# Tower of 16 pairs written out, with keys in SBUF, router results in the projections' bank, one numbered order of PSUM uses and a new order on four engines

## The reference, cut to what matters

```
x = emb[tokens] * sqrt(128) + positions                       # layer 1: additive attention
q, k, v = x @ Wq + bq, x @ Wk + bk, x @ Wv + bv
scores = einsum('d,bijd->bij', attn_scale, tanh(q[:, :, None, :] + k[:, None, :, :]))
x = layer_norm(x + softmax(scores) @ v @ Wo + bo)
x = layer_norm(x + relu(x @ W1 + bf1) @ W2 + bf2)
h = layer 2: causal attention of 8 heads, added to x
h = _ln(x); logits = (h @ Wr) @ codebook.T / 0.7              # layer 3: 64 experts, 2 of them for each token
out = residual + ffn(ln(mixture of 2 experts + shared expert))
```

## Time and profile before

| what | value |
|---|---|
| median of 3 runs | 871.07 us (868.9 to 873.77) |
| span of the profiled execution | 867.1 us |
| its own time | not listed apart from these runs |
| first add of the tower to last add | 12.6 to 544.9 us |
| tower without adds, up to the counts | 544.9 to 626 us |
| experts and last layer | 626 to 867.1 us |
| DVE, ACT, PE busy | 75%, 75%, 89% of the span |

### The profile page before, as it was taken

The page is one execution under the profiler, slowest core; times in us unless marked ns, Lnnn a source line. Parts: engine busy times, 40 slices in busy tenths (PEclk is TensorE's granted clock), DMA queues, the critical chain, the costliest instruction groups (busy, mean ns, idle before and its releaser), DMA issues. The chain is left out here.

```text
span 867.1 us, 22473 instructions
## 1 busy us (share of the span) xinstructions
PE 774.3 (89%) x7235; PEld 593.5 (68%) x7235; DVE 653.6 (75%) x2152; ACT 651.1 (75%) x1487; POOL 324.3 (37%) x396
## 2 busy tenths in 40 slices
PE   2777998888989999999899998988889999999898
PEld 1454676565756766667666675665679999999787
DVE  5999989979999999999999999654533334443685
ACT  3787999979898988998988989766335555565354
POOL 3110322425333353343433533444424645554211
PEclk9999999999999999999999999998899999999999
DMA  3459999999999989898898898997079999996411
GB/s 96 121 110 193 205 188 206 197 189 211 190 197 210 192 195 206 175 211 180 181 208 179 188 197 180 210 185 166 26 228 378 377 395 402 338 363 216 153 30 37
DMA packets 81344, 175.77 MB, mean 203 GB/s; under 512 B 8053, under 2 KB 34764, under 8 KB 81281
## 3 DMA queue, kind: packets, MB, share of 16 engines
q1 hardware_dynamic: 65104, 162.23, 76.1%
q0 software_dynamic: 5664, 7.92, 2.8%
q10 hardware_dynamic: 10512, 4.83, 2.0%
HBM read 63.95 MB, written 113.14 MB: 204 GB/s over the span
## 5 line engine op out<-in xcount | busy, mean ns | idle before, releaser
L893 DVE TENSOR_TENSOR arena<-qT,b_qk 128x2304 f32<-128x2304 f32 x128 | 323.7, 2543 | 1.6 <-DVE v_bias L918 0.3
L624 ACT ACTIVATE arena<-arena 128x2304 f32<-128x2304 f32 x128 | 271.6, 2123 | 35.0 <-DVE arena L893 34.0
L1334 PE MATMUL b_s<-arena,apad 128*32 128x192 f32 x3072 | 159.4, 343 | 27.0 <-ACT p L633 18.5
L1334 PEld LDWEIGHTS b_s<-arena,apad 128*32 128x32 f32 x3072 | 89.8, 113 | 83.9 <-issue 42.0
L779 ACT ACTIVATE act_h<-big,arena 128x128 f32<-128x128 f32 x324 | 92.4, 368 | 72.2 <-PE big L1654 65.6
L544 POOL TENSOR_TENSOR kept<-kept,rs 96x384 f32<-96x384 f32 x64 | 52.6, 823 | 212.6 <-DVE rs L1028 212.4
L592 POOL DMA_INDIRECT eo_dram<-gT,toff x81 | 79.0, 976 | 89.9 <-issue 56.0
L676 ACT ACTIVATE kept<-kept,mx 96x96 f32<-96x96 f32 x256 | 92.3, 365 | 14.5 <-DVE mx L1021 14.5
L1654 PE MATMUL big<-hbT,arena 128*128 128x128 f32 x648 | 86.7, 277 | 6.4 <-DMA arena<-in_wpack 2.4
L1654 PEld LDWEIGHTS big<-hbT,arena 128*128 128x128 f32 x648 | 78.8, 192 | 8.1 <-issue 6.3
L1208 DVE TENSOR_SCALAR hbT<-b_t,cols 128x128 f32<-128x128 f32 x81 | 33.2, 410 | 62.1 <-PE b_t L1647 58.3
(11 more groups left out here) (207 smaller groups left out, 1422.4 us busy)
## 6 DMA issues: line engine op xcount, KB each, us to landing
rows_dram<-act_h SPq DMA_DIRECT2D x32, 3096.0 KB
arena<-in_wpack SPq DMA_DIRECT2D x81, 578.0 KB
prT<-rows_dram ACTq DMA_DIRECT2D x73, 64.5 KB
arena<-eo_dram SPq DMA_DIRECT2D x4, 512.0 KB, 8.1
x_dram<-res SPq DMA_DIRECT2D x16, 96.0 KB
out<-of SPq DMA_DIRECT2D x12, 128.0 KB, 1.8
eo_dram<-gT,toff POOLq DMA_INDIRECT x81
rows_dram<-rows_now,slot_now POOLq DMA_INDIRECT x64
```

The source lines that it names most:

```text
L624: act.activation(v, v, ACT.Tanh).then_inc(s["tanh"], 1)
L893: dve.tensor_tensor(ring[c % TRING].rearrange("p (x m n) -> p x m n", m=CQ, n=N), qv.unsqueeze(3).to_broadcast([D, SPLIT * QG, CQ, N]), kv ...
L1334: last = pe.matmul(b_s[32 * a:32 * a + 32, 0:SPLIT * N], apad[:, 31 - line:63 - line], t[:, :, a, m, :], start=(line == 0), stop=(line == ...
```

## The change

1. **Written out.** `in_turns` calls `body(n)` for all n from -4 to 20; the `Fori` over pairs is gone on PE, ACT, DVE and POOL, and with it register-valued waits and most of the `gate`s (a wait with a semaphore increment of its own behind it). SP keeps its loops. The scatter's slots of all pairs have a column each (`slots`), and the gathers read their index straight from `eidx`, without the copy into `eidx_now`.
2. **Keys in SBUF.** A new ACT stage `keys` copies the 128x192 keys to `kT` with their bias; `queries` on DVE copies the queries behind it. Both tensors have two buffers. `add` reads two SBUF operands. `qk` of the next pair waits for `queries` and no longer for the adds.
3. **Router results in `b_qk`.** Logits and ranks move from `b_y` to `b_qk`.
4. **Banks in a round.** The uses of the three large banks are numbered in PE's order, use i takes bank i mod 3 and waits until use i - 3 has been read. The uses of `b_t` and of `b_y` wait in the same way, each for the use before it.
5. **New orders** on PE, ACT, DVE and POOL, below. The shared expert's first tiles also move.

```diff
-            def qk_evac(p):
-                dve.wait_ge(s["qk"], p + 1)
-                wait(dve, s["add"], p * CH)
-                dve.tensor_scalar(qT[:, :], b_qk[:, 0:TN], bqk[:, :], None, ALU.add).then_inc(s["qk_ev"], 1)
-                dve.wait_ge(s["qk_ev"], p + 1)
+            def queries(p):
+                dve.wait_ge(s["keys"], p + 1)
+                dve.tensor_scalar(qT[:, p % 2, :], p_q, bq, None, ALU.add).then_inc(s["queries"], 1)
 
             def add(p, c):
+                if c == 0:
+                    dve.wait_ge(s["queries"], p + 1)
                 wait(dve, s["score"], p * CH + c - TRING + 1)
                 g, cc = c // CPB, c % CPB
-                kv = p_k[:, g * N:(g + 1) * N]
+                kv = kT[:, p % 2, g * N:(g + 1) * N]
...
+            def keys(p):
+                wait(act, s["add"], (p - 1) * CH)
+                act.wait_ge(s["qk"], p + 1)
+                act.activation(kT[:, p % 2, :], p_k, ACT.Identity, bias=bk).then_inc(s["keys"], 1)
...
-        p_lg = b_y[0:N, 288:288 + G * E].rearrange("p (g e) -> p g e", g=G)
+        p_lg = b_qk[0:N, 0:G * E].rearrange("p (g e) -> p g e", g=G)
...
             def keep_rows(p):
-                if not (known(p) and p == 0):
-                    gate(pool, s["scat"], p * 16 * G * TOPK)
-                gate(pool, s["tn"], p + 1)
+                wait(pool, s["scat"], p * 16 * G * TOPK)
+                pool.wait_ge(s["tn"], p + 1)
...
+            def big_bank(p, what):
+                sem, uses = bank_free(p, what)
+                if uses:
+                    pe.wait_ge(sem, uses)
+                else:
+                    pe.wait_ge(s["raw_ev"], 4)
+                return bank(p, what)
```

POOL's new order, whole (its n is three less than DVE's):

```diff
+                at(n, 3, scatter_rows, 0)
+                at(n, 2, roots_h1)
+                at(n, 1, normalise, 0)
+                at(n, 0, root, "x2")
+                at(n, 1, normalise, 1)
+                at(n, 3, scatter_rows, 1)
+                at(n, -3, keep_x)
+                at(n, -4, gather_emb, 0)
+                at(n, 0, root, "h0")
+                at(n, -4, gather_emb, 1)
+                at(n, 1, normalise, 2)
+                at(n, 1, normalise, 3)
+                at(n, 2, keep_rows)
+                at(n, -1, root, "x1")
```

DVE's new order, whole but for the first pair's setup and the shared expert's stages at the end:

```diff
+                at(n, 5, variance, "h1")
+                at(n, 1, add, 1)
+                at(n, 4, mask_max, 1)
+                at(n, 2, softmax1_max)
+                at(n, 5, h1_norm)
+                at(n, 1, add, 2)
+                at(n, 3, x2_stats)
...
+                at(n, 0, x_rows)
+                at(n, 4, inv_sums, 0)
+                at(n, 3, means, "x2")
+                at(n, 4, mask_max, 2)
+                at(n, 3, variance, "x2")
+                at(n, 3, x2_rows)
+                at(n, 4, inv_sums, 1)
+                at(n, 1, add, 3)
+                at(n, 3, x2_norm)
+                at(n, 2, p1T_copy)
+                at(n, 3, h0_stats)
+                at(n, 4, mask_max, 3)
+                at(n, 5, route)
+                at(n, 3, means, "h0")
+                at(n, 4, inv_sums, 2)
+                at(n, 5, chosen)
+                at(n, 3, variance, "h0")
+                at(n, 1, add, 4)
+                at(n, 2, x1_sums)
+                at(n, 3, xa_norm)
+                at(n, 2, x1_rows)
+                at(n, 1, add, 5)
+                at(n, 5, one_hot)
+                at(n, 2, x1_stats)
+                at(n, 5, both_hot)
+                at(n, 2, means, "x1")
+                at(n, 4, inv_sums, 3)
+                at(n, 5, counted)
+                at(n, 2, variance, "x1")
+                at(n, 1, add, 6)
+                at(n, 5, ranks)
+                at(n, 2, x1_norm)
+                at(n, 1, add, 7)
+                at(n, 4, h1_stats)
+                at(n, 0, queries)
+                at(n, 4, means, "h1")
+                at(n, 3, mask_max, 0)
+                at(n, 0, add, 0)
```

More of the change, by code:

```diff
@@ L62, with wait, in_turns, at_end @@
 MASKED = 1.0e30
-DVE_LINKS = 14
 WCOLS = 2 * DFF + FC + D
 ROWS = ["bo", "g2", "beta2", "bs2", "fbf2"]
+FIRST, PAST = -4, PAIRS + 5
+SHARED_EARLY = 3
+BIG_ORDER = [
[4 rows of a table added]
+]
+T_ORDER = [
+    (3, "x1_turn"), (5, "tn_turn"), (2, "p1_turn"), (3, "xa_turn"), (0, "xs_turn"),
+]
+YA_ORDER = [
+    (3, "ffn2"), (5, "router"), (2, "attend1"), (1, "v_rows"),
+]
+Q_ORDER = [
+    (1, "qk"), (5, "logits"), (5, "ranks"), (5, "shared out 1"),
+]
 def known(value):
     return isinstance(value, int)
[L74 to L97, removed]
+def wait(eng, sem, value):
+    if value > 0:
+        eng.wait_ge(sem, value)
+def in_turns(body):
+    for n in range(FIRST, PAST):
         body(n)
 def at(n, k, stage, *which):
-    p = n - k
-    if not known(p) or 0 <= p < PAIRS:
-        stage(p, *which)
+    if 0 <= n - k < PAIRS:
+        stage(n - k, *which)
+def at_end(n, k, stage, *which):
+    if n - k == PAIRS - 1:
+        stage(*which)
+def numbered(order):
+    found = {}
+    for n in range(FIRST, PAST):
+        for k, what in order:
+            if 0 <= n - k < PAIRS and (n - k == PAIRS - 1 or not what.startswith("shared")):
+                found[what, n - k] = len(found)
+    return found
+BIG_USE, T_USE, YA_USE = (numbered(order) for order in (BIG_ORDER, T_ORDER, YA_ORDER))
+Q_USES = list(numbered(Q_ORDER))
+Q_USE = {use: i for i, use in enumerate([use for use in Q_USES if use[0] in ("logits", "ranks")])}
+for j in range(SHARED_EARLY, NB - SHARED_LATE):
+    BIG_USE[f"shared {j}", PAIRS - 1] = len(BIG_USE)
 def program(nc, io, out):
@@ L567, in body @@
             def body(n):
[L568 to L583, removed]
+                at(n, 3, scatter_rows, 0)
[12 more added lines that the diff above has]
+                at(n, -1, root, "x1")
+            in_turns(body)
             def store_rows(t):
@@ L911, in setup @@
             def setup(p):
-                if not (known(p) and p == 0):
+                if p:
                     return
@@ L1336, in score, with q_bank_free @@
                 last.then_inc(s["score"], 1)
+            def big_bank(p, what):
[5 more added lines that the diff above has]
+                return bank(p, what)
+            def q_bank_free(p, what):
+                use = Q_USES.index((what, p))
+                if use:
+                    before, of = Q_USES[use - 1]
+                    if before == "qk":
+                        pe.wait_ge(s["queries"], of + 1)
+                    elif before in ("logits", "ranks"):
+                        pe.wait_ge(s["q_ev"], Q_USE[before, of] + 1)
+                    else:
+                        pe.wait_ge(s["ysh"], 2)
             def xs_turn(p):
+                wait(pe, s["t_ev"], T_USE["xs_turn", p])
                 pe.wait_ge(s["xs"], p + 1)
```

594 lines of the change are left out of this document (265 added, 329 removed), and 10 rows, old and new, of tables (BIG_ORDER, s).

## The result

The changed kernel takes **928.08 us** (median of 4 runs, 920.12 to 931.9) against 870.39 for the kernel before on the same chip (4 runs): a ratio of 1.0648, 95% interval 1.0593 to 1.0703, or +57.7 us. The prediction had the sign but not the size: it said +17.4 (888.5), and its range ended at 902.

A forecast was written before the change was run, and what follows sets the result against it. DVE, the fullest engine, was taken as the bound: a period is its work plus its waits. Eleven pairs +14.0, head +2, last pair +1, start +0.4 gave +17.4 us: span 884.5, time 888.5, range 848 to 902.

The forecast's parts named there:

- the mechanism that decides: DVE adds with two SBUF operands hold POOL's instructions for whole instructions, and held POOL work then delays DVE.
- The walk: One period stepped through in DVE's and POOL's new orders: DVE's waits for held POOL work sum to 3.8 us a pair.
- Head and start: Before the eleven pairs: +2 us for the head (-4 to +5) and +0.4 us once for the keys copy.
- The add's own time: Each DVE add with keys in SBUF: change of 0 to -0.03 us, +-0.1 allowed, taken as 0.
- Writing out and the router's bank: Loop written out: 0.2 us a pair, inside the eleven-pair figure; router results in b_qk: 0.
- The 4 us that I put between span and time: Added to the forecast span of 884.5 us to give the time of 888.5 us.
- The wait for the projections: DVE's wait once a pair, because adds read keys in PSUM: 0.8 us, forecast to go.
- all else is late-proof: PE and ACT have 3 to 4 us to spare, so a period is DVE's 33.1 + 3.8 = 36.9 us.
- My third rival: Delayed normalises push PE's transposes and the round of banks passes it on: 1 us more a pair, 900 us; chance 0.06.
- matmuls at an unchanged price: PE's busy time a pair taken as before: 32.3 us at full clock, 33.3 where the granted clock is 0.95.
- the right case: Expected signs of held adds: add maximum above 3 us, DVE busy near 36 us a period, a period of 37 us.
- a cause priced at nothing: Sign of being wrong: DVE busy 33 us and waiting on PE's large banks, priced at 0.

The follow-up runs named there:

- e2: Kernel before, plus a DVE copy of the keys to SBUF each pair, which the adds read: 981.48 us, ratio 1.1288.
- e3: Control on the kernel before: same DVE copy of the keys to SBUF, but the adds still read PSUM: 871.63 us, ratio 1.0027.
- e5: Changed kernel with router results back in their old bank and v_copy ahead of prT_copy 2 on ACT; keys stay in SBUF: 927.35 us, ratio 1.0641.
- e1: e5 with the adds reading keys in PSUM, the keys copy gone, and qk waiting for the previous pair's adds: 902.46 us, ratio 1.0365.
- e12: Changed kernel with PE's transpose pr_turn 2 moved later, behind heads_g 0, xs_turn and score 3: 895.29 us, ratio 1.0279.
- e4: Kernel before with its hardware loop over pairs written out, nothing else changed: 873.36 us, ratio 1.0024.
- e6: e1 with PE's qk moved behind attend2 3, so that it comes after the adds: 886.38 us, ratio 1.0114.
- e10: Changed kernel with PE's ranks moved up, right behind heads_g 0: 932.33 us, ratio 1.069.
- e15: e12 with PE's transpose pr_turn 0 also moved, behind router and score 0: 896.14 us, ratio 1.0286.

## Why the prediction was right or wrong

**Right: the mechanism that decides.** POOL's instructions are held by adds with two SBUF operands; e2 against e3 and e5 against e1 show it. The price on DVE was nearly right too. The walk said 3.8 us a pair. In the changed kernel DVE waits 2.3 us a pair for roots (1.6 + 0.7) and is busy 34.1 us a pair (374.66 over eleven) instead of the 33.1 that I took: 3.3 us. In e12 it is 2.9 of waits and, in the pair shown, 1.4 of busy time (34.5): 4.3. The items differ: the roots of h0 cost 1.6 where I had 0.6, and no add was ever delayed, where I had 0.6 before add 6.

**Right: the small terms.** Head and start: +2.9 against +2.4 (the last pair's adds cost +4.9, where I had +1; they stand in the same regime). The add's own time: 2546 ns against 2544, no change. Writing out and the router's bank: within 0.5%, by e4 and by e5 against the changed kernel. The 4 us that I put between span and time hold 1.9 us that every run shows and 2 us by which the profiled execution was faster than the median run. The wait for the projections went, as forecast.

**Wrong: the step "all else is late-proof (PE and ACT have 3 to 4 us to spare)".** I held PE's stages against the pair's length, not against what is queued behind a stand. PE takes its stages in order, comes to `pr_turn` 2 while POOL's `normalise` is held, and stands 2.9 us; `ranks` is the sixth stage behind it, and DVE waits there 4.0 us in the mean, plus 0.6 for scores. In us a pair: 34.1 busy + 2.3 roots + 4.0 + 0.6 = 41.0; the eleven pairs took 40.7 each (447.3 / 11), where I had 36.9. e12 shows that one stand, with the low clock behind it, to be 33 us of the time; with it moved the kernel takes 895.3 us, 7 us above the forecast. My third rival named this very path (delayed `normalise`s push PE's transposes), but at 1 us a pair and a chance of 0.06; it cost more than four times that, and I had not walked PE's order as I had walked DVE's.

**Wrong with it: matmuls at an unchanged price.** I took PE's 32.3 to 33.3 us a pair over. In the pair shown PE is busy 35.7, and the granted clock falls to 0.50 twice in it, behind the stand at `pr_turn` 2 and behind one of 1.97 us at `pr_turn` 0. I hadn't priced that a stand makes the work behind it dearer. No run separates the stand from the clock; the two kinds of pairs do in part: with the stand the same, 0.67 us more wait makes the pair 0.67 us longer. In the timeline shown, the stand is 2.9 us, and the six groups of matmuls from the turn to `ranks` last 7.3 us together, where the same forms at full clock last 4.8: 2.5 us more. Of these 5.4 us DVE waits 4.45. In the pairs with the later fall, 3.4 us of matmuls run at half clock, which is 1.7 us more (an estimate from the stretch 278.98 to 282.40).

**Wrong, size not separated: POOL's indirect DMAs.** My walk has no item for them. They are held too: the scatters of rows take 0.94 us or up to 3.7, a gather of embeddings up to 3.4. POOL is busy 28.5 us a pair, twice the 14.2 of e1.

**Wrong signs in my own list.** I wrote that the right case would show adds over 3 us and DVE busy near 36 us. Adds have a maximum of 2.66 and DVE 34: the adds aren't held, and the holding appears mostly as DVE's waits. A part is in its busy time, 34.0 us a pair against 32.8 in e1, since short operations of DVE are held by POOL's. The largest item, in the changed kernel and in e1 (whole span):

```profile
L1029 DVE SCALAR_TENSOR_TENSOR h<-xg,rstd_x,row_beta x32: 335/808/816, 73.8 to 642.1; 96x128 f32<-96x128 f32 x32
```

```profile
L1024 DVE SCALAR_TENSOR_TENSOR h<-xg,rstd_x,row_beta x32: 335/338/809, 75.0 to 612.3; 96x128 f32<-96x128 f32 x32
```

DVE busy little more than 33 us and waiting on PE, near to what I had named as a cause priced at nothing, is what came; but it waits for `ranks` (4.0 us a pair) and hardly for the large banks (0.6).

**What stays open.** The new order costs 1% with keys in PSUM (e6), through waits between DVE and PE in both directions; which stages these need in another place was not settled. No run kept the stands at a full clock either, so what the clock costs of the 33 us is an estimate. Which part the held indirect DMAs have in it wasn't tested.

## What to carry to other kernels

Before moving an operand of a long VectorE operation from PSUM to SBUF, look at what GpSimd does meanwhile: here eight adds a pair held it up for whole instructions, 110 us in an order that wasn't made for it, while the add gained nothing. When an engine is delayed, follow the delay through every in-order queue that waits for it, and ask at each stand what is queued behind it and who needs that; spare time of an engine over a period is no protection. A wait that shows up last is cured at the stand where it began: moving the late stage (e10) gained nothing, moving the stage that stood (e12) 33 us. Not every stand costs: moving a second one (e15) gained nothing more.

## What was not expected of the hardware

- **A long add hardly ever gives way, short operations of DVE often do** (L1029 above). In the changed kernel no add of 2.5 us did (2517 to 2656 ns over 128), though POOL's instruction can be on record before it. Timeline of POOL and DVE around 302 us in the changed kernel:

```profile
301.90 3.52 POOL L569 TENSOR_TENSOR rstd_x<-ve_x,halves 96x2 f32<-96x2 f32 x1
```

```profile
302.34 2.52 DVE L921 TENSOR_TENSOR arena<-qT,kT 128x2304 f32<-128x2304 f32 x1
305.55 1.07 DVE L1029 SCALAR_TENSOR_TENSOR h<-xg,rstd_x,row_beta 96x128 f32<-96x128 f32 x2 [0.69 <-POOL rstd_x L569]
```

  The root is recorded 0.44 us before the add, ends 0.56 us after it, and holds the next DVE operation in turn (1.07 us). The Trainium skill, "SBUF — State Buffer", section "SBUF: two separate sides", says that whichever of the two starts first gets the ports for the whole instruction; by the recorded starts this root would have been first. The measurement decides here: it was the root that waited. Whether its request for the ports comes later than its recorded start, no run shows. In e2 two adds in 128 did wait (3.14 and 3.08 us):

```profile
L895 DVE TENSOR_TENSOR arena<-qT,kT x128: 2517/2548/3136, 12.8 to 648.5; 128x2304 f32<-128x2304 f32 x128
```

  At the first, POOL's `keep_x` is on record 0.02 us before the add (23.52 us) and took its usual 0.73. The second add stands directly behind another one, and `keep_x`, held by that one (95.93 to 98.97 us), got in between the two.
- **Indirect DMAs on POOL are held as well**, at these adds with two SBUF inputs: 0.94 us became up to 3.74 (line L597 above).
- **A stand of some 2 us on PE brought as long a stretch of half clock as one of 2.5 us, and the length of the stand alone doesn't decide.** In the changed kernel each of the 21 stands of 1.96 to 2.90 us between 126 and 574 us has a stretch at 0.50 that begins within it or up to 1.4 us behind it. It lasts 3.4 us, or 6.8 where it begins within the stand. In e12 seven of nine stands of 2.5 us have one; the other two, which end at 172.84 and 476.59 us, have none until a stand of 1.32 us some 4 us later. In the kernel before, PE stands 1.17 us at the same stage of each pair, and of five such stands from 240 to 390 us three have the stretch.
- **A PSUM operand costs a long add nothing**: 2544 ns with the keys in PSUM, 2546 in SBUF.
